# Softmax attention: the values of a unit summed in four pieces, each between two scores, in place of one

## The reference

```python
x = x + _L0_attn_ref(_layernorm(x, axis=-1), Wq, Wk, Wv, Wo)      # x: 2 x 1024 x 512
# inside, 32 query heads and 8 key/value heads of 16 columns each, every key/value head serves 4 query heads:
scores = jnp.einsum('bqhd,bkhd->bhqk', xq, xk) / math.sqrt(HEAD_DIM)
scores = jnp.where(causal[None, None], scores, -jnp.inf)
probs = jax.nn.softmax(scores.astype(jnp.float32), axis=-1)
out = jnp.einsum('bhqk,bkhd->bqhd', probs, xv).reshape(b, s, N_HEADS * HEAD_DIM)
return out @ Wo
```

## Time and profile before

| | |
|---|---|
| median of the runs | 3093.97 us |
| the profiled execution | 3091.87 us |
| its span, first to last instruction | 3090.1 us |
| TensorE busy | 2953.2 us, 96% of the span |
| VectorE, ScalarE, GpSimd busy | 1598.5, 1440.7, 1413.1 us |
| granted TensorE clock, mean | 0.98 |

### The profile page before, as it was taken

How to read it: one execution, slowest core, us unless ns; L and a number is a source line. 1 busy time by engine, 2 the same in 40 slices (tenths; PEclk the granted TensorE clock), 3 DMA queues, 4 the chain that set the end, 5 groups by cost and what they waited for, 6 DMA issues and landing times. The chain is left out here.

```text
span 3090.1 us, 54423 instructions
## 1 busy us (share of the span) xinstructions
PE 2953.2 (96%) x18200; PEld 2350.5 (76%) x18200; DVE 1598.5 (52%) x2742; ACT 1440.7 (47%) x2510; POOL 1413.1 (46%) x1243
## 2 busy tenths in 40 slices
PE   7799999989999999999999989999999999999958
PEld 6444444358888888888888878888888888888846
DVE  6677777637444444334444446434444443444478
ACT  5266666644444444444444444444444444444421
POOL 5411111122555555555555554554555555455531
PEclk9799999999999999999999998999999999999979
DMA  4411212002111111111111120111111111111121
GB/s 142 120 27 28 40 27 40 15 32 72 45 37 44 44 37 44 48 44 37 44 44 37 44 95 28 46 53 38 39 49 37 37 48 51 37 42 47 52 87 55
DMA packets 102712, 149.58 MB, mean 48 GB/s; under 512 B 24228, under 2 KB 44452, under 8 KB 102376
## 3 DMA queue, kind: packets, MB, share of 16 engines
q1 hardware_dynamic: 102632, 148.52, 16.5%
HBM read 129.74 MB, written 18.35 MB: 48 GB/s over the span
## 5 line engine op out<-in xcount | busy, mean ns | idle before, releaser
L1860 PE MATMUL bank<-l_xC,l_w_T 128*128 128x512 f32 x2304 | 561.9, 393 | 0.0
L1860 PEld LDWEIGHTS bank<-l_xC,l_w_T 128*128 128x128 f32 x2304 | 428.1, 188 | 87.9
L1860 PE MATMUL bank<-l_xT,l_w_T 128*128 128x512 f32 x1728 | 453.2, 401 | 6.5 <-DVE l_gT L1753 6.5
L789 DVE TENSOR_REDUCE att_max<-bank 128x1 f32<-128x640 f32 (+6 forms) x352 | 354.7, 1027 | 107.0 <-PE bank L829 103.4
L752 ACT ACTIVATE att_exp<-bank 128x512 f32<-128x512 f32 x576 | 323.6, 596 | 148.8 <-PE bank L844 142.7
L1753 DVE TENSOR_TENSOR l_kT<-bank,l_qT 128x512 f32<-128x512 f32 x128 | 88.5, 692 | 577.8 <-PE bank L1860 577.8
L1829 PEld LDWEIGHTS bank<-l_v_T,l_xT 128*128 128x128 f32 x3072 | 376.5, 191 | 7.4 <-issue 5.0
L1829 PE MATMUL bank<-l_v_T,l_xT 128*128 128x256 f32 x3072 | 377.8, 285 | 4.4 <-PEq L1013 2.7
L1860 PEld LDWEIGHTS bank<-l_xT,l_w_T 128*128 128x128 f32 x1728 | 310.6, 188 | 69.6 <-DVE l_gT L1753 12.7
L1875 PE MATMUL bank<-l_o_T,l_y_hi 128*128 128x512 f32 x1024 | 324.1, 393 | 0.0
L1595 POOL TENSOR_TENSOR l_qd<-l_qT,l_q_decay 128x1024 f32<-128x1024 f32 x64 | 151.9, 2373 | 372.7 <-ACT l_qT L1658 372.7
(11 more groups left out here) (281 smaller groups left out, 5067.1 us busy)
## 6 DMA issues: line engine op xcount, KB each, us to landing
l_w_raw<-in_L_attn_qkv_w SPq DMA_DIRECT2D x196, 256.0 KB, 2.8
l_w_raw<-in_L_attn_gate_w SPq DMA_DIRECT2D x66, 256.0 KB, 2.7
l_o_raw<-in_L_attn_out_w SPq DMA_DIRECT2D x33, 512.0 KB, 3.5
query_parts<-att_exp SPq DMA_DIRECT2D x48, 128.0 KB
att_QT<-query_parts SPq DMA_DIRECT2D x16, 384.0 KB, 5.5
X<-x_rows SPq DMA_DIRECT2D x3, 2048.0 KB, 13.6
X<-in_L_attn_x SPq DMA_DIRECT2D x4, 1024.0 KB, 11.2
att_QT<-query_parts SPq DMA_DIRECT2D x16, 256.0 KB, 5.5
```

Of the source, the lines that this page charges most:

```text
L789: dve.tensor_reduce(mx[:, g % 2, heads[0]:heads[-1] + 1, q], columns(slot, q, len(heads), step), AX_X, ALU.max).then_inc(s_read, 1)
L1860: mm = pe.matmul(ps_p[p_bank(event)][:, :], w[:, SLOT[pair], LEFT[i], P * c:P * c + P], quarter(i, x, xc, c), start=(n == 0 and i in (1, 6 ...
```

## The change

The event `("values", U)` becomes four events `("values", U, j)`, one for each head. They stand at U + 2.725 + j/4, which is always between two scores, since those stand at multiples of a quarter. The function takes the head as an argument, its waits are made by the first piece alone, and the last piece raises `pv_done`. The events keep and back move with it, as their last piece is at U + 3.475.

```diff
-        placed += [(U + 1 + VALUES_LAG, 2, ("values", U)) for U in range(ALL)]
+        placed += [(U + 1.1 + VALUES_LAG + j / REP, 2, ("values", U, j)) for U in range(ALL) for j in range(REP)]
         for G in range(GROUPS):
-            summed = [NU * G + HALF_DONE[half] + 1 + VALUES_LAG for half in range(2)]
-            placed += [(summed[half] + 1.1, 3, ("keep", G, half)) for half in range(2)]
-            placed.append((summed[1] + 1.6, 4, ("back", G)))
+            summed = [NU * G + HALF_DONE[half] + 1.75 + VALUES_LAG for half in range(2)]
+            placed += [(summed[half] + 0.5, 3, ("keep", G, half)) for half in range(2)]
+            placed.append((summed[1] + 1.0, 4, ("back", G)))
...
-                def times_v(U):
+                def times_v(U, j):
 
                     g, u = divmod(U, NU)
-                    pe.wait_ge(e_ready, REP * U + REP)
-                    pe.wait_ge(causal, diagonals(U + 1))
+                    if j == 0:
+                        pe.wait_ge(e_ready, REP * U + REP)
+                        pe.wait_ge(causal, diagonals(U + 1))
                     a = 0
                     for key, q, count in UNITS[u]:
                         half = q // HALF
-                        if key == 0 and g >= 1:
+                        if key == 0 and g >= 1 and j == 0:
                             pe.wait_ge(kept, 2 * (g - 1) + half + 1)
                         b, c = a + count * P, (q % HALF) * P
                         first = (SEQ_TILES * g + key) * V_COLS
-                        for j in range(REP):
-                            mm = pe.matmul(ps_oT[half][WIDE * j:WIDE * (j + 1), c:c + b - a], V[:, first:first + WIDE],
-                                           E[:, U % RING, j, a:b], start=(key == 0), stop=(u == HALF_DONE[half]),
-                                           skip_group_check=True)
+                        mm = pe.matmul(ps_oT[half][WIDE * j:WIDE * (j + 1), c:c + b - a], V[:, first:first + WIDE],
+                                       E[:, U % RING, j, a:b], start=(key == 0), stop=(u == HALF_DONE[half]),
+                                       skip_group_check=True)
                         a = b
-                    mm.then_inc(pv_done, 1)
+                    if j == REP - 1:
+                        mm.then_inc(pv_done, 1)
...
                     if event[0] == "values":
-                        times_v(event[1])
+                        times_v(*event[1:])
```

## The result

The changed kernel takes 3503.55 us (median of four runs, 3502.74 to 3505.27), the kernel before 3092.38 us (3090.43 to 3095.16). The ratio is 1.133 with an interval of 1.131 to 1.135. The forecast was 3490 us, and the range 3430 to 3540.

A forecast was written before the change was run, and what follows sets the result against it. TensorE was taken to bound the kernel. From 3091.9 us, 565 single pieces at 1.05 us replacing 142 events at 1.08 add 440 us, and hidden waits give back 42: 3490 us, range 3430 to 3540.

The forecast's parts named there:

- The mechanism: On TensorE, scores between heads stop four heads running side by side; each piece costs an event; path grows by 440 us.
- The piece at 1.05 us: A single values piece on TensorE: 0.08 in, 0.43 between passes, 0.54 out; 565 pieces make 593 us.
- The waits given back: TensorE's short waits in the attention, for exponentials and for VectorE, are all hidden by the longer path: 42 us less.
- The two switches: Going into and out of quarter-width work on TensorE costs each single piece 0.08 in and about 0.1 out.
- the sum without them, 3388 us: Rival: the switches vanish for single pieces, so a piece costs 0.87 us and the kernel 3388 us; chance 0.03.
- The covers: Moved keep and back, exponentials and group loads add no wait; if one failed, a few tenths of a us per group.
- the ring of five units: Exponentials of unit U + 5 wait for U's last piece, issued a unit and a half ahead of their score: nothing added.
- The end of the stage: The last 11 pieces, joined behind the last score, take about 2.1 us inside the existing 2.46 us wait.
- A lone pass: Rival: a lone head streams faster on TensorE, a pass 0.22 and a piece 0.63 us, giving 3253 us; chance 0.05.
- the second pass's weights: Rival: they are not loaded in the first pass's shadow, 0.11 us more per piece, giving 3552 us; chance 0.04.
- the clock: Rival: TensorE's clock falls to its lower level, the stage takes 1770 us, the kernel about 4370 us; chance 0.02.
- the marks named: Timeline signs: values line busy about 590 us, ScalarE's score waits some 500 us, ScalarE and VectorE busy times unchanged.

The follow-up runs named there:

- The pairs: Changed kernel with two pieces per unit in place of four, heads 0 and 1 together, heads 2 and 3 together: 3199.8 us.
- The full-width kernel: Changed kernel with 128 columns of V as weights in place of 32, so every values matmul has full width: 3403.8 us.
- the kernel with double events: Kernel before, with the values of two neighbouring units placed at one point, 72 double events in place of 144: 3107.8 us.

## Why the prediction was right

**The mechanism.** It is the one forecast. Four heads side by side cost what one costs, and a full-width score between them puts them one behind another. The sign and size follow from the price of an event. Joined pieces are back at 3095, two events in a unit give 3200, four give 3504, all by one price: (3199.8 - 3092.0 + 43) / 141 = 1.07 and (3503.6 - 3092.4 + 43) / 423 = 1.07 us for each added event. Keeping the heads in one quarter without any score in between already costs 369 us, so it is the serialisation and not the order that is paid for.

**The piece at 1.05 us.** This is the term that was mis-sized, by 0.02, and its split was not quite mine. The first distance of a lone piece is 0.45 (706.33 to 706.78) and not 0.43: with all heads in one quarter, too, the first is 0.45 and the next 0.43, so the longer one belongs to the first pass behind the change of shape and not to the neighbours. But the second distance is 0.52 and not 0.54, and the two together are the 0.97 of the forecast, or 0.98 in other pieces. The way in is 0.09 (0.32 less 0.23) where I took 0.08. So a piece is 1.06 to 1.07. With 1.07, 565 pieces are 605 us and the sum is 3501, against 3503.4 for the profiled execution. The group says the same: 57.5 us against 56.9, with 36 x 0.02 = 0.7. Of the 13 us by which that execution lies above 3490, about 10 are this term; the 3.9 behind the attention were not forecast at all.

**The waits given back.** All of the waits went, as forecast: TensorE has no idle time from 165 to 1050 us, and the group's 57.5 us are its work by starts with nothing left for waits (28.8 less 9.7 for the nine events of before, and 36 x 1.07, make 57.6). My 29 us for the 14.2 steady groups is a slip, 14.2 x 2.0 are 28, so the waits are 41 rather than 42; this moves nothing else. The reason is the one given, work between the scores, and the experiment with one quarter shows that without it a longer path gives nothing back. The pairs show that it need not stand between any two of them.

**The two switches.** Taken as 0.18 for each piece and belonging to the shape. The full-width kernel measured 0.177 for both, so the sum without them, 3388 us, would have been wrong. Of the added 454 us (411 and the 43 given back), 423 x 0.18 = 76 are switches and the rest streaming.

**The covers.** Keep, back, the ring of five units and the loads cost nothing that can be seen. The end of the stage is as forecast: from the last score at 1050.38 to the last unit's values at 1052.85 there are 2.47 us, where there were 2.46.

**The rivals.** A lone pass is not faster than four at once (0.45 and 0.43, not 0.22); the second pass's weights cost nothing (0.45 from pass to pass, as with four heads); the clock stayed at 1.00 from 165 to 1050 us. Of the marks named, the values line covers 589.6 us (590 forecast), ScalarE waits 534.6 us for scores (about 500), and the busy times of VectorE and ScalarE stayed within 2%.

## What to carry to other kernels

Matmuls that use a quarter of the array's columns are cheap only while they stand next to one another in different quarters; before cutting such a group, divide the wall time of the group, not the mean of its records, by its members. A cut costs one whole event, here 1.07 us, of which 0.18 is the way in and out of the shape. Waits between neighbours are hidden by work that stands between them, and work moved there can wait itself for the engine that reads it.

## What the runs showed that I had not expected

Quarter-width work of one head written wholly ahead of the next head's still overlaps: sixteen records of a two-block unit take 1.02 us. A full-width float32 matmul that wastes three quarters of its output is cheaper than the same work in a quarter, 0.86 to 0.91 against 1.07 us, when it stands alone among full-width work. Waits between scores were gone already with an event in every second gap. And the kernel with double events lost TensorE's clock (0.67 over 10 us) behind a wait of 1.71 us that the kernel before has as well and went through at 1.00.
